# A recurrent decoder layer: both decay weights' arguments from one difference of running maximum and key, positive parts and parameters moved from VectorE to ScalarE

## The chip, the cores and the metric

The kernel runs on one core of one Trainium2 chip. The metric is the device time of one execution in microseconds (us), lower is better; times of a kernel are given as the median of several runs.

## What is computed

The program is one decoder block: four recurrent (RWKV) layers over x of 16 x 112 x 256 (batch, tokens, channels), then linear attention against a context of 16 x 375 x 256, then a dense mixture of eight experts. The change touches the recurrent layers only, in the recurrence that the reference calls wkv. Cut to that:

```python
w = -jnp.exp(time_decay); u = time_first          # one number per channel and layer
def step(carry, kv):
    aa, bb, pp = carry                            # numerator, denominator, running maximum
    kk, vv = kv
    ww = u + kk
    qq = jnp.maximum(pp, ww)
    e1 = jnp.exp(pp - qq); e2 = jnp.exp(ww - qq)
    out = (e1 * aa + e2 * vv) / (e1 * bb + e2)
    ww2 = pp + w
    qq2 = jnp.maximum(ww2, kk)
    e1b = jnp.exp(ww2 - qq2); e2b = jnp.exp(kk - qq2)
    return ((e1b * aa + e2b * vv, e1b * bb + e2b, qq2), out)
```

Around it each layer has two layer norms, three input mixes with their projections (key k, value v, gate r), an output projection, and a channel part (a hidden layer of 1024 with squared relu, and a gate).

## The kernel before

**Layout and steps.** The 16 sequences are cut into four groups of four. A group's working tiles are 128 channels x 2 channel halves (`CB`) x 4 sequences x 112 tokens, that is 128 partitions x 896 numbers, float32; an operation that needs a number per channel (bias, scale) has to be issued once per half, 128 x 448. Four layers by four groups are 16 units of work, m = 0 to 15; m // 4 is the layer. The order of the work is written out by hand, separately for each engine, in one loop over s = 0 to 16: while the channel part of unit s runs, the mixes, projections and recurrence of unit s + 2 are done, and the first norm of unit s + 3. Engines meet only through semaphores; each engine executes its own list strictly in order, so whatever waits holds back all that is behind it. Three warm-up units stand ahead of the loop.

**The recurrence of one unit** (lines 343 to 403 on VectorE, 652 to 671 on ScalarE). `pp` is the running maximum, made by one scan over the keys `kp` (L352). Then VectorE forms three arguments: `dp`, old maximum minus new maximum (L355); `dk`, key minus new maximum (L356); and `du` = key + u - old maximum (L359, one instruction per channel half because u differs by channel; it is put into the tile `rw`). ScalarE makes of them `e1b` = exp(dp + w) (L656, one per half, w as the bias), `e2b` = exp(dk) (L659), and `eu` = exp(u + key - old maximum), held below exp(24), as a Relu (L662) and an Exp (L664), each over the whole tile. VectorE's `wkv_sums` waits for e1b and e2b and runs the two scans `bb` (L366) and `aa` (L370); `wkv_denominator` (L375) waits for `eu`.

**The lists around it, in iteration s.**
- ScalarE, from the gate on: `gate(s)` (cth, L679, waits for TensorE's product with `wcr`), a table load (L761), `rsqrt0(1, s+3)` (L583, L585), `hidden(s, 0)` (L632, L634, L636: relu, square, rounded copy kfh), e1b, e2b of unit s + 2, `hidden(s, 1)`, `hidden(s, 2)`, a norm (L610 x4), eu, `hidden(s, 3)`, and then, in iteration s + 1, `rsqrt0(2, s+1)`: L583 `lnv` and L585 `y`.
- VectorE: `wkv_out`, `wkv_arguments` (L352 to L359), in some iterations a weight residue (L433, L440), `low_kf(s, 0)` (L421: the low part of the hidden values, kfl), the norm's four small operations (L274 to L286), `wkv_sums` (L366, L368, L370), `low_kf(s, 1)`, `low_kf(s, 2)`; then in iteration s + 1 `add_wkv` (L409), statistics (L268), the denominator (L375), L382, L383, the four small operations of the second norm (L274 waits for ScalarE's `y`), and `low_kf(s, 3)` (L421).
- TensorE, iteration s + 1: output projection `wo` (L809), the channel output in four quarters of 24 matmuls (L839; quarter p waits for kfl number p), with a transpose (L789) between, a second transpose, three projections (L799), the gate product `wcr` (L809), the hidden layer (L824).

So the fourth quarter of L839 can't start before VectorE's last `low_kf`, which stands behind L274, which waits for ScalarE's `y`, which stands behind all exponentials and hidden values of that iteration.

Layers' weights make the iterations differ by s % 4. When s % 4 is 0 (from s = 4 on) VectorE also computes two weight residues and ScalarE two weight copies (L643); at 2 and 3 one of each; at 1 none.

`prm` is the tile of the parameters per channel, with the columns of `NAMES`; columns from "w" on are computed at the start (L466 to L472 and L685).

Of the kernel before, what the change touches and what calls it, by code (L numbers as in the profile page):

```python
# [8 lines left out]
ACT = mybir.ActivationFunctionType  # L9
# [3 lines left out]
B, T, C = 16, 112, 256  # L13
L, F = 4, 1024
CB = C // P
# [3 lines left out]
T1 = T + 1  # L19
EPS = 1e-5  # L20
NEVER = -1e38
MOST = 24.0
UNIT = -0.5 / C
LN_EXP, EXP_TANH = "natural_log_exp_and_others", "exp_and_others"
FT = F // P
NAMES = ["ln1w", "ln1b", "tmk", "tmv", "tmr", "td", "u", "ln2w", "ln2b", "cmk", "cmr", "w", "pmk", "pmr"]
PRM = {n: i for i, n in enumerate(NAMES)}
NPRM, NPRM_IN = len(NAMES), NAMES.index("w")
S = 375
# [49 lines left out]
def rwkv_phase(nc, g, io, ctx):  # L79
# [11 lines left out]
    with tiles:  # L91
        def sb(name, shape, dt=FP32):
            return tiles.enter_context(nc.sbuf_tensor(name, shape, dt))

        def sem(name):
            return ctx.enter_context(nc.semaphore(name))
# [12 lines left out]
        prm = sb("prm", [P, L, CB, NPRM])  # L109
        eps, most = sb("eps", [P, 1]), sb("most", [P, 1])  # L110
# [18 lines left out]
        t = sb("kfl", [P, FT, G * T], F32R)  # L129
# [8 lines left out]
        kp = sb("kp", [P, CB, G, T1])  # L138
        v = sb("v", [P, CB, G, T])
        th = sb("th", [P, CB, G, T])  # L140
        pp = sb("pp", [P, CB, G, T1])
        reset = sb("reset", [P, G, T1])
        decay = sb("decay", [P, CB, G, T1])
        dp, dk = sb("dp", [P, CB, G, T]), sb("dk", [P, CB, G, T])
        diff = dk
        rw = [sb(f"rw{i}", [P, CB, G, T]) for i in range(2)]
        eu = sb("eu", [P, CB, G, T])
        e1b, e2b = sb("e1b", [P, CB, G, T1]), sb("e2b", [P, CB, G, T1])
# [8 lines left out]
        wexp_done, w_ready = sem("wexp_done"), sem("w_ready")  # L157
# [15 lines left out]
        arg_ready, side_ready, exp_ready = sem("arg_ready"), sem("side_ready"), sem("exp_ready")  # L173
# [72 lines left out]
        def vector(dve):  # L246
# [3 lines left out]
            def did(ins):  # L250
                ins.then_inc(dve_step, 1)
                steps[0] += 1
                return steps[0]

            def after(n):
                dve.wait_ge(dve_step, n)
# [5 lines left out]
            def param(m, b, name):  # L262
                return prm[:, m // GROUPS, b, PRM[name]:PRM[name] + 1]
# [33 lines left out]
            def input_stats(m):  # L297
                dve.wait_ge(x_in[m], 16)
                if m >= 2:

                    dve.wait_ge(shift_ready[0], m - 1)
                stats(0, chunk(m))
# [30 lines left out]
            def flat(t):  # L333
                return t[:].rearrange("p b g t -> p (b g t)")

            def at(t, first):

                return t[:, :, :, first:first + T].rearrange("p b g t -> p (b g) t")

            def tokens(t):  # L340
                return t[:].rearrange("p b g t -> p (b g) t")

            def wkv_arguments(m):
                n = 0
                if m % GROUPS == 0:
                    for b in range(CB):

                        n = did(dve.tensor_scalar(decay[:, b], reset[:], param(m, b, "w"), None, ALU.add))
                    after(n)
                dve.wait_ge(k_out, m + 1)  # L350

                n = did(dve.tensor_tensor_scan(flat(pp), flat(decay), flat(kp), 0.0, ALU.add, ALU.max))  # L352
                du = rw[m % 2]
                after(n)
                dve.tensor_tensor(tokens(dp), at(pp, 0), at(pp, 1), ALU.subtract).then_inc(arg_ready, 1)  # L355
                dve.tensor_tensor(tokens(dk), at(kp, 1), at(pp, 1), ALU.subtract).then_inc(arg_ready, 1)  # L356
                for b in range(CB):

                    dve.scalar_tensor_tensor(du[:, b], kp[:, b, :, 1:T1], param(m, b, "u"),  # L359
                                             pp[:, b, :, 0:T], ALU.add, ALU.subtract).then_inc(arg_ready, 1)  # L360

            def wkv_sums(m):


                dve.wait_ge(exp_ready, 4 * m + 3)
                did(dve.tensor_tensor_scan(flat(bb), flat(e1b), flat(e2b), 0.0, ALU.mult, ALU.add))  # L366
                dve.wait_ge(v_out, m + 1)
                n = did(dve.tensor_tensor(at(aa, 1), at(e2b, 1), tokens(v), ALU.mult))  # L368
                after(n)
                did(dve.tensor_tensor_scan(flat(aa), flat(e1b), flat(aa), 0.0, ALU.mult, ALU.add))  # L370

            def wkv_denominator(m):

                dve.wait_ge(exp_ready, 4 * m + 4)
                dve.tensor_tensor(tokens(dp), tokens(eu), at(bb, 0), ALU.add).then_inc(den_ready, 1)  # L375

            sums = {}
# [85 lines left out]

            dve.wait_ge(wexp_done, 1)
            pw = PRM["w"]
            dve.tensor_scalar(prm[:, :, :, pw:pw + 1], prm[:, :, :, pw:pw + 1], -1.0, None, ALU.mult).then_inc(w_ready, 1)  # L466
            for name in ("ln1w", "ln2w"):
                p = PRM[name]
                dve.tensor_scalar(prm[:, :, :, p:p + 1], prm[:, :, :, p:p + 1], UNIT, None, ALU.mult).then_inc(w_ready, 1)
            for name, mu in (("pmk", "cmk"), ("pmr", "cmr")):  # L470
                p, c = PRM[name], PRM[mu]
                dve.tensor_scalar(prm[:, :, :, p:p + 1], prm[:, :, :, c:c + 1], -1.0, 1.0, ALU.mult, ALU.add)\  # L472
                    .then_inc(w_ready, 1)
            dve.wait_ge(w_ready, 5)
            input_stats(0)
            rsqrt(0, 0)
            after(normalise(0, chunk(0)))
# [34 lines left out]
            for s in range(STEPS + 1):  # L512
# [40 lines left out]
                if valid(s + 2):  # L553
                    wkv_arguments(s + 2)
# [16 lines left out]
        def scalar(act):  # L571
            context_first, attention = g["attention"]["scalar"](act)

            def param(m, b, name):
                return prm[:, m // GROUPS, b, PRM[name]:PRM[name] + 1]
# [4 lines left out]
            def rsqrt0(k, m):  # L580

                act.wait_ge(lnstat[k], G // 2 * (m + 1))
                act.activation(lnv[k][:], m2[k], ACT.Ln, bias=eps[0:T, :], scale=1.0 / C).then_inc(lnlog[k], 1)  # L583
                act.wait_ge(lnlog[k], m + 1)
                act.activation(y0[k][:], lnv[k][:], ACT.Exp, scale=-0.5).then_inc(lny0[k], 1)  # L585
# [64 lines left out]
                act.activation(low[name][LOW[l][0]], stage[name][:, 0:HALF], ACT.Copy).then_inc(early_ready, 1)  # L650

            def wkv_exp(m, what):
                act.wait_ge(arg_ready, 4 * m + (what + 1 if what < 2 else 4))
                if what == 0:
                    for b in range(CB):
                        act.activation(e1b[:, b, :, 1:T1], dp[:, b], ACT.Exp, bias=param(m, b, "w"))\  # L656
                            .then_inc(exp_ready, 1)
                elif what == 1:
                    act.activation(e2b[:, :, :, 1:T1], dk[:], ACT.Exp).then_inc(exp_ready, 1)  # L659
                else:  # L660

                    act.activation(eu[:], rw[m % 2][:], ACT.Relu, bias=most[:], scale=-1.0).then_inc(side_ready, 1)  # L662
                    act.wait_ge(side_ready, m + 1)
                    act.activation(eu[:], eu[:], ACT.Exp, bias=most[:], scale=-1.0).then_inc(exp_ready, 1)  # L664

            def reciprocal0(m):
# [6 lines left out]
            def gate(m):  # L673

                act.wait_ge(cr_done, m + 1)
                if m:
# [5 lines left out]
            act.wait_ge(const_set, 12)  # L682
            act.wait_ge(params_in, 48)
            act.preload_act_table_set(LN_EXP)
            act.activation(prm[:, :, :, PRM["w"]:PRM["w"] + 1], prm[:, :, :, PRM["td"]:PRM["td"] + 1],  # L685
                           ACT.Exp).then_inc(wexp_done, 1)
            act.wait_ge(w_ready, 5)
            rsqrt0(0, 0)
            high_weights(0, "ck", wckh, ck_done, 4)
            rsqrt0(1, 0)  # L690
# [90 lines left out]
        def tensor(pe):  # L781
# [64 lines left out]
            for s in range(-3, STEPS + 1):  # L846
# [43 lines left out]
                if valid(m):  # L890
# [19 lines left out]
                    hidden(m, 3)  # L910

        return {"gpsimd": gpsimd, "sync": sync, "vector": vector, "scalar": scalar, "tensor": tensor}

def attention_phase(nc, g, io, ctx):
# [1172 lines left out]
```

## Time and profile before

| | us |
|---|---|
| median of 3 runs | 1837.98 (1837.52 to 1838.78) |
| the profiled execution's own time | 1839.21 |
| its span in the profile | 1837.5 |
| busy in the span: TensorE / VectorE / ScalarE | 1736.6 / 1242.6 / 977.0 |
| end of the recurrent layers in the profile | about 700 |

How to read it: the span is the time between first and last recorded instruction; the execution's own time is 1.7 us longer, what lies around the span. "Busy" sums recorded durations. In the profile's slices of the span VectorE is busy nine tenths or more in the recurrent part and about half in the experts; ScalarE's share falls likewise. A timeline row gives start, length, engine, line, and in brackets how long the engine had been idle before it and which engine and line released it. The length of a row that joins two instructions runs from the first's start to the second's end; instructions that follow each other on one engine overlap by about 0.1 us.

### The profile page before, as it was taken

Reading aid. Unit: us, or ns where it says so; the run is one execution under the profiler, and the core shown is the slowest. Engines: PE = TensorE matmul, PEld = TensorE weight load, DVE = VectorE, ACT = ScalarE, POOL = GpSimd, SP = SyncE. Lnnn points to the kernel's source line nnn. Section 1 sums busy time; section 2 is a strip of 40 time slices with the busy share of each in tenths; the row PEclk is TensorE's granted clock in tenths of the full one; section 3 lists DMA queues with packets and bytes.
Section 4 is the critical chain, followed back from the end, with each engine's and each line's share of the span. In section 5 each row is a group of like instructions: output and inputs, shape, how many; then the busy total and the mean of one; then the engine's idle time right before and its main releaser. Section 6 shows DMA issues by size and latency. Waiting matters only on the chain.

```text
span 1837.5 us, 27225 instructions
## 1 busy us (share of the span) xinstructions
PE 1736.6 (95%) x10508; PEld 1520.3 (83%) x10508; DVE 1242.6 (68%) x1918; ACT 977.0 (53%) x1505; POOL 3.6 (0%) x26
## 2 busy tenths in 40 slices
PE   3599999999999998998999999999999999999997
PEld 1378888778888788888899889998999989999896
DVE  7999999999999855888554445444454544445446
ACT  4688898898989773444533333333333332333323
POOL 0000000000000000000000000000000000000000
PEclk9799999999999998999999999999999999999999
DMA  4000010001000002111111010000011001120001
GB/s 143 1 25 17 12 47 18 7 8 62 1 12 29 0 30 89 44 55 45 55 35 35 1 35 35 34 33 2 34 34 34 11 23 34 34 74 0 1 1 41
DMA packets 34702, 56.59 MB, mean 31 GB/s; under 512 B 3030, under 2 KB 20412, under 8 KB 33596
## 3 DMA queue, kind: packets, MB, share of 16 engines
q1 hardware_dynamic: 34620, 55.47, 9.3%
q8 instruction: 55, 0.90, 0.2%
q14 instruction: 27, 0.22, 0.0%
HBM read 51.79 MB, written 3.67 MB: 30 GB/s over the span
## 4 chain that ended last, share of the span: by engine, by line
PE 70%; DVE 24%; ACT 3%; issue 2%; DMA 0%; SPq 0%; ACTq 0%; DVEq 0%
PE fbank L1935 33%; PE fbank L1957 17%; PE pair L839 5%; PE pair L799 4%; PE pair L824 3%; DVE kfl L421 2%; PE proj L1429 2%; PE pair L809 2%; DVE st L268 2%; DVE aa L370 1%; DVE bb L366 1%; DVE pp L352 1%; PE qbanks L1465 1%; PE pair L789 1%; DVE x L409 1%
## 5 line engine op out<-in xcount | busy, mean ns | idle before, releaser
L1757 DVE TENSOR_TENSOR hf<-sil,fbank 128x512 f32<-128x512 f32 (+1 forms) x256 | 158.8, 620 | 479.2 <-PE fbank L1935 407.5
L1862 ACT ACTIVATE sil<-fbank 128x512 f32<-128x512 f32 (+1 forms) x256 | 139.2, 544 | 615.1 <-PE fbank L1935 615.1
L1935 PE MATMUL fbank<-xh,wh 128*128 128x512 f32 (+1 forms) x1024 | 289.8, 364 | 1.2 <-ACT sil L1862 1.2
L1935 PE MATMUL fbank<-xl,wh 128*128 128x512 f32 (+1 forms) x1024 | 289.0, 363 | 0.0
L1935 PE MATMUL fbank<-xh,wl 128*128 128x512 f32 (+1 forms) x1024 | 288.9, 363 | 0.0
L1957 PE MATMUL fbank<-wl,hh 128*128 128x256 f32 x896 | 250.3, 279 | 0.0
L1957 PE MATMUL fbank<-wh,hh 128*128 128x256 f32 x896 | 250.2, 279 | 0.0
L1957 PE MATMUL fbank<-wh,hl 128*128 128x256 f32 x896 | 250.1, 279 | 0.0
L1935 PEld LDWEIGHTS fbank<-xl,wh 128*128 128x128 f32 x1024 | 184.6, 189 | 30.8
L1935 PEld LDWEIGHTS fbank<-xh,wl 128*128 128x128 f32 x1024 | 184.4, 189 | 30.4
L1935 PEld LDWEIGHTS fbank<-xh,wh 128*128 128x128 f32 x1024 | 180.5, 189 | 27.8 <-ACT sil L1862 1.6
L1957 PEld LDWEIGHTS fbank<-wl,hh 128*128 128x128 f32 x896 | 168.3, 188 | 2.1
L1957 PEld LDWEIGHTS fbank<-wh,hh 128*128 128x128 f32 x896 | 168.4, 188 | 1.8
L1957 PEld LDWEIGHTS fbank<-wh,hl 128*128 128x128 f32 x896 | 168.4, 188 | 0.0
L1764 DVE TENSOR_TENSOR hl<-hf,hh 128x512 fp32r<-128x512 f32 (+1 forms) x256 | 158.1, 618 | 0.0
L839 PE MATMUL pair<-wcvh,kfh 128*112 128x256 f32 x512 | 148.7, 291 | 9.8 <-DVE kfl L421 9.2
L1855 ACT ACTIVATE hh<-hf 128x512 fp32r<-128x512 f32 (+1 forms) x256 | 146.0, 570 | 0.5 <-DVE hf L1757 0.5
L839 PE MATMUL pair<-wcvh,kfl 128*112 128x256 f32 x512 | 143.8, 281 | 0.0
L839 PE MATMUL pair<-wcvl,kfh 128*112 128x256 f32 x384 | 107.6, 280 | 0.0
L839 PEld LDWEIGHTS pair<-wcvh,kfh 128*112 128x112 f32 x512 | 89.7, 175 | 13.5 <-DVE kfl L421 12.8
L839 PEld LDWEIGHTS pair<-wcvh,kfl 128*112 128x112 f32 x512 | 89.7, 175 | 0.0
L1781 DVE SCALAR_TENSOR_TENSOR acc<-fbank,cw,acc 128x256 f32<-128x256 f32 x210 | 87.3, 475 | 0.0
(239 smaller groups left out, 3109.6 us busy)
## 6 DMA issues: line engine op xcount, KB each, us to landing
raw<-in_w_gate SPq DMA_DIRECT2D x16, 512.0 KB, 3.8
raw<-in_w_up SPq DMA_DIRECT2D x16, 512.0 KB, 4.7
raw<-in_w_down SPq DMA_DIRECT2D x16, 512.0 KB, 5.7
raw<-in_w_ck SPq DMA_DIRECT2D x4, 1024.0 KB, 4.8
raw<-in_w_cv SPq DMA_DIRECT2D x4, 1024.0 KB, 4.8
raw<-in_ctx_t SPq DMA_DIRECT2D x4, 750.0 KB, 5.9
ct<-in_ctx_t SPq DMA_DIRECT2D x4, 750.0 KB, 4.9
x<-in_x SPq DMA_DIRECT2D x4, 448.0 KB, 6.9
```

Source lines behind the costliest of these rows:

```text
L268: dve.bn_stats(st[k][:, i, :], xc[:, 2 * i:2 * i + 2, :].rearrange("p g c -> p c g"))\
L421: dve.tensor_tensor(kfl[j], kf[j], kfh[:, 2 * j:2 * j + 2], ALU.subtract)\
L799: ins = pe.matmul(pair[KVR[which]][:, o, 0:G * T], w[:, b, o * P:(o + 1) * P], src[:, b].rearrange("p g t -> p (g t)"), start=b == 0, stop ...
L824: ins = pe.matmul(banks[:, i, 0:G * T], w[b], a[:, b, :], start=n == 0, stop=n == 3 * CB - 1)
L839: ins = pe.matmul(pair[3][0:T, i // 2, (i % 2) * C:(i % 2 + 1) * C], a[:, i * T:(i + 1) * T], w, start=j == n == i % 2 == 0, stop=j == FT ...
L1757: dve.tensor_tensor(hf[i][:, 0:w], sil[i][:, 0:w], banks(e, t, f)[1][:, 0:w], ALU.mult).then_inc(hf_ready, 1)
L1764: dve.tensor_tensor(hl[t % 2][:, f, 0:w], hf[f % 2][:, 0:w], hh[t % 2][:, f, 0:w], ALU.subtract)\
L1781: ins = dve.scalar_tensor_tensor(a, ps, w, a, ALU.mult, ALU.add)
L1855: act.activation(hh[t % 2][:, f, 0:w], hf[f % 2][:, 0:w], ACT.Copy).then_inc(hh_ready, 1)
L1862: act.activation(sil[f % 2][:, 0:w], banks(e, t, f)[0][:, 0:w], ACT.Silu).then_inc(sil_ready, 1)
L1935: ins = pe.matmul(banks(e, t, f)[k][:, 0:w], m[h][:, o:o + P], a[:, b, columns(c)], start=i == 0, stop=i == 3 * CB - 1)
L1957: ins = pe.matmul(bank[4 + 2 * (t % 2) + i // 2][:, (i % 2) * C:(i % 2 + 1) * C], a[t % 2][:, f, i * P:(i + 1) * P], m[h][:, DOWN + f * C: ...
```

## The change

On VectorE, `dp` becomes old maximum minus key, and `du` is no longer computed (two instructions less for each unit). On ScalarE both e1b and eu start from dp. With we = exp(time_decay) = -w, the new maximum is the larger of old maximum + w and key, so the argument of e1b is -max(0, we - dp): one Relu for each half with bias we and scale -1, then one Exp with scale -1 over the whole tile. The argument of eu is 24 - max(0, 24 - u + dp): one Relu for each half with bias 24 - u, then the Exp as before. The semaphores' counts follow. At the start one more small VectorE instruction makes the column 24 - u.

```diff
-NAMES = ["ln1w", ..., "cmr", "w", "pmk", "pmr"]
+NAMES = ["ln1w", ..., "cmr", "w", "we", "mostu", "pmk", "pmr"]
...
                 n = did(dve.tensor_tensor_scan(flat(pp), flat(decay), flat(kp), 0.0, ALU.add, ALU.max))
-                du = rw[m % 2]
                 after(n)
-                dve.tensor_tensor(tokens(dp), at(pp, 0), at(pp, 1), ALU.subtract).then_inc(arg_ready, 1)
+                dve.tensor_tensor(tokens(dp), at(pp, 0), at(kp, 1), ALU.subtract).then_inc(arg_ready, 1)
                 dve.tensor_tensor(tokens(dk), at(kp, 1), at(pp, 1), ALU.subtract).then_inc(arg_ready, 1)
-                for b in range(CB):
-                    dve.scalar_tensor_tensor(du[:, b], kp[:, b, :, 1:T1], param(m, b, "u"),
-                                             pp[:, b, :, 0:T], ALU.add, ALU.subtract).then_inc(arg_ready, 1)
...
-                dve.wait_ge(exp_ready, 4 * m + 3)
+                dve.wait_ge(exp_ready, 3 * m + 2)
...
-                dve.wait_ge(exp_ready, 4 * m + 4)
+                dve.wait_ge(exp_ready, 3 * m + 3)
...
-            dve.tensor_scalar(prm[:, :, :, pw:pw + 1], prm[:, :, :, pw:pw + 1], -1.0, None, ALU.mult).then_inc(w_ready, 1)
+            pe, pu, pm = PRM["we"], PRM["u"], PRM["mostu"]
+            dve.tensor_scalar(prm[:, :, :, pw:pw + 1], prm[:, :, :, pe:pe + 1], -1.0, None, ALU.mult).then_inc(w_ready, 1)
+            dve.tensor_scalar(prm[:, :, :, pm:pm + 1], prm[:, :, :, pu:pu + 1], -1.0, MOST, ALU.mult, ALU.add)\
+                .then_inc(w_ready, 1)
...
             def wkv_exp(m, what):
-                act.wait_ge(arg_ready, 4 * m + (what + 1 if what < 2 else 4))
+                def over(out, name, scale):
+                    for b in range(CB):
+                        act.activation(out[:, b], dp[:, b], ACT.Relu, bias=param(m, b, name), scale=scale)\
+                            .then_inc(side_ready, 1)
+                per = 2 * CB
                 if what == 0:
-                    for b in range(CB):
-                        act.activation(e1b[:, b, :, 1:T1], dp[:, b], ACT.Exp, bias=param(m, b, "w"))\
-                            .then_inc(exp_ready, 1)
+                    act.wait_ge(arg_ready, 2 * m + 1)
+                    t = e1b[:, :, :, 1:T1]
+                    over(t, "we", -1.0)
+                    act.wait_ge(side_ready, per * m + CB)
+                    act.activation(t, t, ACT.Exp, scale=-1.0).then_inc(exp_ready, 1)
                 elif what == 1:
+                    act.wait_ge(arg_ready, 2 * m + 2)
                     act.activation(e2b[:, :, :, 1:T1], dk[:], ACT.Exp).then_inc(exp_ready, 1)
                 else:
-                    act.activation(eu[:], rw[m % 2][:], ACT.Relu, bias=most[:], scale=-1.0).then_inc(side_ready, 1)
-                    act.wait_ge(side_ready, m + 1)
+                    over(eu, "mostu", 1.0)
+                    act.wait_ge(side_ready, per * (m + 1))
                     act.activation(eu[:], eu[:], ACT.Exp, bias=most[:], scale=-1.0).then_inc(exp_ready, 1)
```

What the engines' lists show. VectorE after the scan `pp` of unit 3 (iteration s = 1), before:

```order
L355 TENSOR_TENSOR dp<-pp 128x896 [waits dve_step]
L356 TENSOR_TENSOR dk<-kp,pp 128x896
L359 SCALAR_TENSOR_TENSOR rw<-kp,prm,pp 128x448 x2
L421 TENSOR_TENSOR kfl<-kf,kfh 128x896 [waits kfh_ready]
L274 TENSOR_TENSOR yy<-y 112x4 [waits lny01]
```

and now:

```order
L354 TENSOR_TENSOR dp<-pp,kp 128x896 [waits dve_step]
L355 TENSOR_TENSOR dk<-kp,pp 128x896
L416 TENSOR_TENSOR kfl<-kf,kfh 128x896 [waits kfh_ready]
L274 TENSOR_TENSOR yy<-y 112x4 [waits lny01]
```

The two half-tile instructions that made `du` are gone; nothing else moves. ScalarE between the first hidden values and the second, same iteration, before:

```order
L636 ACTIVATE kfh<-kf 128x896 [waits square_done]
L656 ACTIVATE e1b<-dp,prm 128x4x112 [waits arg_ready]
L656 ACTIVATE e1b<-dp,prm 128x4x112
L659 ACTIVATE e2b<-dk 128x8x112 [waits arg_ready]
L632 ACTIVATE kf<-pair 128x896 [waits ck_done]
```

and now:

```order
L634 ACTIVATE kfh<-kf 128x896 [waits square_done]
L654 ACTIVATE e1b<-dp,prm 128x4x112 [waits arg_ready]
L654 ACTIVATE e1b<-dp,prm 128x4x112
L663 ACTIVATE e1b<-e1b 128x8x112 [waits side_ready]
L666 ACTIVATE e2b<-dk 128x8x112 [waits arg_ready]
L630 ACTIVATE kf<-pair 128x896 [waits ck_done]
```

One whole-tile Exp, which waits for the two Relus (`side_ready`), now stands ahead of e2b. Further down the eu pair, before:

```order
L610 ACTIVATE xn<-x,shift,rstd 112x256 x3
L662 ACTIVATE eu<-rw,most 128x896 [waits arg_ready]
L664 ACTIVATE eu<-eu,most 128x896 [waits side_ready]
L632 ACTIVATE kf<-pair 128x896 [waits ck_done]
```

and now:

```order
L608 ACTIVATE xn<-x,shift,rstd 112x256 x3
L654 ACTIVATE eu<-dp,prm 128x448 x2
L670 ACTIVATE eu<-eu,most 128x896 [waits side_ready]
L630 ACTIVATE kf<-pair 128x896 [waits ck_done]
```

The whole-tile Relu has become two of half the size. TensorE's list is the same.

## Rows read from the trace of the kernel before

**Rows 1.** Busy time in one whole layer: stretch, each engine's busy us, clock
```profile
285.18:443.12 157.94, 155.15 (x865) 128.51 (x865) 153.10 (x199) 139.55 (x189) 0.00 (x0) 1.00 0.07 22
```
**Rows 2.** TensorE timeline: first matmul of the fourth L839 quarter, s % 4 = 0, 1, 2, 3
```profile
281.33 0.37 PE L839 MATMUL pair<-wcvh,kfh 128*112 128x256 f32 x1 [1.63 <-DVE kfl L421]
...
319.90 0.37 PE L839 MATMUL pair<-wcvh,kfh 128*112 128x256 f32 x1
...
359.62 0.37 PE L839 MATMUL pair<-wcvh,kfh 128*112 128x256 f32 x1 [0.93 <-DVE kfl L421]
...
556.38 0.37 PE L839 MATMUL pair<-wcvh,kfh 128*112 128x256 f32 x1
```
**Rows 3.** Waits between 200 and 660 us: total us, times, longest
```profile
ACT cth L679 <- PE pair L809: 20.4, 9, 2.9
...
DVE mix_ck L330 <- ACT mix_ck L601: 3.9, 11, 0.4
```
**Rows 4.** Chain of waits: VectorE's du pair
```profile
538.06 1.19 DVE rw L359 x2
```
**Rows 5.** Groups of instructions, ScalarE, to 800 us: busy us, mean ns
```profile
L656 ACT ACTIVATE e1b<-dp,prm 128x448 f32<-128x448 f32 x32 | 19.5, 656 | 2.6 <-DVE dp L355 2.6
...
L671 ACT ACTIVATE e1b<-e2b 128x896 f32<-128x896 f32 x16 | 15.3, 955 | 0.5
```
**Rows 6.** ScalarE timeline, iteration s = 5 (s % 4 = 1)
```profile
303.27 1.22 ACT L656 ACTIVATE e1b<-dp,prm 128x448 f32<-128x448 f32 x2
304.39 0.95 ACT L659 ACTIVATE e2b<-dk 128x896 f32<-128x896 f32 x1
...
312.74 1.03 ACT L662 ACTIVATE eu<-rw,most 128x896 f32<-128x896 f32 x1
313.80 1.05 ACT L664 ACTIVATE eu<-eu,most 128x896 f32<-128x896 f32 x1
...
317.85 0.20 ACT L585 ACTIVATE y<-lnv 112x4 f32<-112x4 f32 x1
```
**Rows 7.** VectorE timeline, iteration s = 5
```profile
305.37 2.04 DVE L366 TENSOR_TENSOR_SCAN bb<-e1b,e2b 128x904 f32<-128x904 f32 x1 [0.21 <-ACT e2b L659]
...
318.09 0.16 DVE L274 TENSOR_TENSOR yy<-y 112x4 f32<-112x4 f32 x1
...
318.76 1.08 DVE L421 TENSOR_TENSOR kfl<-kf,kfh 128x896 fp32r<-128x896 f32 x1
```
**Rows 8.** y and the L274 behind it: s = 4, 6, 11 (s % 4 = 0, 2, 3)
```profile
277.07 0.20 ACT L585 ACTIVATE y<-lnv 112x4 f32<-112x4 f32 x1
279.53 0.15 DVE L274 TENSOR_TENSOR yy<-y 112x4 f32<-112x4 f32 x1
...
356.44 0.20 ACT L585 ACTIVATE y<-lnv 112x4 f32<-112x4 f32 x1
357.82 0.16 DVE L274 TENSOR_TENSOR yy<-y 112x4 f32<-112x4 f32 x1
...
554.07 0.20 ACT L585 ACTIVATE y<-lnv 112x4 f32<-112x4 f32 x1
554.58 0.15 DVE L274 TENSOR_TENSOR yy<-y 112x4 f32<-112x4 f32 x1
```
**Rows 9.** The same two instructions in iteration s = 0
```profile
120.07 0.20 ACT L585 ACTIVATE y<-lnv 112x4 f32<-112x4 f32 x1
121.64 0.15 DVE L274 TENSOR_TENSOR yy<-y 112x4 f32<-112x4 f32 x1
```
**Rows 10.** Warm-up, units 0 and 1: e2b and the scan bb behind it
```profile
38.91 0.94 ACT L659 ACTIVATE e2b<-dk 128x896 f32<-128x896 f32 x1
40.51 2.03 DVE L366 TENSOR_TENSOR_SCAN bb<-e1b,e2b 128x904 f32<-128x904 f32 x1
...
67.75 0.93 ACT L659 ACTIVATE e2b<-dk 128x896 f32<-128x896 f32 x1
70.66 2.04 DVE L366 TENSOR_TENSOR_SCAN bb<-e1b,e2b 128x904 f32<-128x904 f32 x1
```

More of the change, by code:

```diff
@@ L25 @@
 FT = F // P
-NAMES = ["ln1w", "ln1b", "tmk", "tmv", "tmr", "td", "u", "ln2w", "ln2b", "cmk", "cmr", "w", "pmk", "pmr"]
+NAMES = ["ln1w", "ln1b", "tmk", "tmv", "tmr", "td", "u", "ln2w", "ln2b", "cmk", "cmr", "w", "we", "mostu", "pmk", "pmr"]
 PRM = {n: i for i, n in enumerate(NAMES)}
@@ L473, in vector @@
                     .then_inc(w_ready, 1)
-            dve.wait_ge(w_ready, 5)
+            dve.wait_ge(w_ready, 6)
             input_stats(0)
@@ L684, in scalar @@
             act.preload_act_table_set(LN_EXP)
-            act.activation(prm[:, :, :, PRM["w"]:PRM["w"] + 1], prm[:, :, :, PRM["td"]:PRM["td"] + 1],
+            act.activation(prm[:, :, :, PRM["we"]:PRM["we"] + 1], prm[:, :, :, PRM["td"]:PRM["td"] + 1],
                            ACT.Exp).then_inc(wexp_done, 1)
-            act.wait_ge(w_ready, 5)
+            act.wait_ge(w_ready, 6)
             rsqrt0(0, 0)
```

## The prediction

> **What bounds the kernel now.** I read the busy times by stretch first. In one whole layer of 157.94 us TensorE is busy 155.15, VectorE 153.10 and ScalarE 139.55, at a granted clock of 1.00 [rows 1]. By that table VectorE is nearly full and relieving it should pay, but TensorE is nearly full too. So the second view is TensorE's timeline, for where it stands still. It does so in one place of an iteration, ahead of the fourth quarter of L839, and always for VectorE's last kfl: 1.63 us when s % 4 is 0, 0.93 when it is 2, under the list's threshold at 1 and 3 (at 3 the start at 556.38 is still the end of kfl) [rows 2]. Those gaps are the most that a faster VectorE could win in the loop. The third view is the waits: ScalarE's gate L679 waits for TensorE's product in nine iterations, and VectorE's mix_ck for ScalarE in eleven [rows 3]. So once per iteration both are set back to TensorE's time, and what they save or lose before that goes on only through the kfl for which TensorE waits. I therefore follow one chain: TensorE's gate product, ScalarE from gate through hidden values and exponentials to the norm's y (L585), VectorE's L274, last kfl, TensorE.
>
> **What is removed.** VectorE's du pair takes 1.19 us of each of 16 units [rows 4]. In the loop it stands ahead of L366, which waits for e2b. In s = 5 e2b ends at 304.39 + 0.95 = 305.34 and L366 starts at 305.37 [rows 6, 7]: there VectorE is waiting already, and the saving is nothing. dp reads another tile in the same shape; I cost that at nothing, since its start is hidden behind ScalarE's hidden values: e1b starts only at 303.27.
>
> **What is added on ScalarE.** First e1b. Before: two half-tile Exps, and e2b starts 1.12 after the first (303.27, 304.39) [rows 6]. Now two half-tile Relus with a bias from a tile, as the old Exps had (0.656 each, 1.22 together) [rows 5, 6], then an Exp that waits for them, then e2b. A dependent instruction starts some 0.03 after the end of what it reads (L664 at 313.80, after 312.74 + 1.03) [rows 6]. An Exp over the whole tile without a bias tile takes 0.955, as L671 [rows 5], and the next starts about 0.09 before its end (two of 0.656 take 1.22 [rows 5, 6]). So e2b starts 1.22 + 0.03 + 0.86 = 2.11 after the first Relu, 0.99 later than before. Second eu. Before: the Exp starts 1.06 after the Relu (312.74, 313.80) [rows 6]; now 1.22 + 0.03 = 1.25 after the first of two: 0.19 more. Together ScalarE gets 1.18 us longer between gate and y, in each unit. Bounds: if the Exp starts without the dependency's wait and overlaps fully, and the eu halves cost only the extra overlap, 1.0; if the Exp costs like L664 (1.05) [rows 6] and both dependencies 0.05 more, 1.37.
>
> The Trainium skill, "ScalarE: Activation LUTs", section "Rules for kernel authors", says to run relu, add and mul on VectorE and not here, which speaks against the change. The rows don't show the reason it gives (speed per element): half a tile costs 1.19 / 2 = 0.60 on VectorE and 0.56 to 0.66 here. By either price the work is about even; what decides is whose time is waited for.
>
> **Iteration by iteration.** L274 starts about 0.04 after y's end (317.85 + 0.20, 318.09), and the last kfl starts 0.67 after it and takes 1.08: 319.84, when TensorE starts at 319.90 [rows 2, 6, 7]. With y 1.18 later:
> - **s % 4 = 1** (1, 5, 9, 13). L274 waits for y already, so all 1.18 arrives. In some of the four TensorE had a few hundredths in hand, and in the last the norm on ScalarE falls away and only e1b's 0.99 counts; I take 1.1 each: +4.4.
> - **s % 4 = 2** (2, 6, 10). y's end goes from 356.64 to 357.82, L274 from 357.82 to 357.86 [rows 8]. VectorE's own saving is eaten by e2b and eu on the way. +0.04 each: +0.1.
> - **s % 4 = 3** (3, 7, 11). y's end goes from 554.27 to 555.45, L274 from 554.58 to 555.49 [rows 8]: +0.9 each, +2.7.
> - **s % 4 = 0** (4, 8, 12). Here VectorE is late because of two weight residues. y's end goes from 277.27 to 278.45, L274 from 279.53 to 278.49 [rows 8]: -1.04 of the 1.63 that TensorE waits, and VectorE's own 1.19 allows it. -3.1.
> - **s = 0**: y's end from 120.27 to 121.45, L274 from 121.64 to 121.49 [rows 9]: -0.15.
>
> The loop's sum is 4.4 + 0.1 + 2.7 - 3.1 - 0.15 = +3.95. Each of these lets gate, mix_ck and the projections move with TensorE, so the terms add.
>
> **Warm-up.** TensorE and ScalarE have much idle time there, VectorE sets the pace. Unit 0: e2b ended at 39.85 and L366 started at 40.51, after the du pair. Now e2b ends at 40.84, so L366 comes 0.36 later [rows 10]. The added instruction on 8 numbers per partition costs 0.1 more. Unit 1 then starts 0.45 late: e2b ends at 68.68 + 0.45 + 0.99 = 70.12, L366 starts at 70.15, where it stood at 70.66, since the du pair no longer fills the time [rows 10]. So the loop begins 0.5 us earlier. Nothing in attention or experts is touched; they move with the end of the recurrence.
>
> **Sum.** 3.95 - 0.5 = **+3.4 us**: 1842.6 for the profiled execution of 1839.21, which stood 1.2 above the median of 1837.98. Against the median the forecast is **1841.4 us**, 0.19% slower. A measurement of this kernel can tell about 0.2% (3.7 us) from no change, so the likeliest result lies just inside that border.
>
> **Rivals.**
> - **The VectorE saving passes through (faster).** If the Relus and the Exp overlap so that e2b comes no later, L366 and L274 start up to 1.19 earlier and TensorE wins what it waited: 1.19 at s % 4 = 0, 0.93 at 2, up to 0.3 at 3, nothing at 1, some 2.4 a layer, 7 in three layers, about 1.2 at s = 0 and 2.4 in the warm-up. That gives -11: 1827. For it: VectorE's 97% [rows 1]. Against it: L366 releasing directly on e2b in s = 5 [rows 7], with an Exp more in front. 5 in 100. The Trainium skill, "Perfetto Trace Analysis", "Identifying the Most-Contended Engine", would point here: optimise the engine of highest occupancy first. By busy time that is VectorE rather than ScalarE's 88%, and the trace agrees on the shares; it disagrees on who is waited for.
> - **ScalarE's chain is dearer (clearly slower).** The place is the pair Relu, Exp on e1b in place, in strided rows, and the same on eu. At 1.5 instead of 1.18 each of 14 iterations gives 0.32 more: +4.5, together +7.9, 1845.9. It decides early: 0.02 us more for each iteration carries the result over 3.7 us. For it: no row shows a Relu of half a tile out of VectorE's tile with its Exp behind it. Against: L656, L662 and L671 are that form in everything but one point each [rows 5, 6]. 10 in 100.
> - **ScalarE's addition is cheaper.** At 0.8 instead of 1.18, -0.38 in 14 iterations is -5.3: -1.9, 1836. It would need the Exp to cost 0.6. 7 in 100.
>
> **How the numbers follow.** The forecast's case has 78 in 100. Inside it the bounds 1.0 and 1.37 give 14 x -0.18 = -2.5 and 14 x 0.19 = +2.7, so 1838.9 to 1844.1, and 46 in 100 of it lie beyond +3.7. Slower by over 0.2%: 0.78 x 0.46 + 0.10 = 0.46. Faster: 0.05. Within 0.2%: the rest, 0.42 + 0.07 = 0.49. The range goes from 1837.3 (half the way into the cheap case) to 1844.9 (half the way into the dear one); the faster case and the ends of both others are left out.
>
> **What the profile after should show.** VectorE's busy time in the span down by about 32 x 0.6 = 19 us or a little more, ScalarE's up by about 20 (0.955 for the Exp and 0.28 for a Relu in two halves, 16 times). VectorE waits for e2b ahead of L366 in nearly every iteration, for about 1 to 2 us, and for y ahead of the second norm's L274 in all. TensorE's wait ahead of the fourth L839 quarter: 0.6 (1.63 - 1.04) at s % 4 = 0, 1.1 at 1, 1.0 at 2, 1.2 at 3; its wait in all becomes more even. A whole layer takes 157.94 + 0.04 + 0.9 + 1.15 - 1.04 = about 159 us. Three things would prove me wrong: L366 starting without a wait; e2b starting less than 2.0 or more than 2.3 after the first Relu; iterations with s % 4 = 1 not growing.

## The result, and the profile after

The change makes the kernel slower by 0.3%: 1844.13 us (median of 9 runs, 1842.28 to 1844.80) against 1837.98 (9 runs, 1836.29 to 1839.11), ratio 1.0032 with an interval of 1.0023 to 1.0042. The forecast was 1841.4, inside a range of 1837.3 to 1844.9. So the sign was right, and the size was 6.2 us where 3.4 was forecast. The forecast gave 46 in 100 to a result slower by over 0.2%, which is what came, and 49 to one within 0.2%. A second comparison (after_again, below) gave 1842.23.

The profiled execution took 1844.8 us (span 1842.7; before 1839.21 and 1837.5). What lies outside the span has grown too: 2.1 us in each of the 16 runs of the changed kernel (2.04 to 2.14), where 54 runs of the kernel before in the later comparisons have 1.7 (1.67 to 1.80). du_kept and e1b_only, which keep the du pair, have 1.7 as well, and the kernels without it 1.9 to 2.2, so these 0.4 us go with its removal; why, no run shows. Section 1 of the page after, and the chain that ended last by engine, followed by that chain on the page before:

```profile
PE 1738.1 (94%) x10508; PEld 1519.7 (82%) x10508; DVE 1226.3 (67%) x1887; ACT 994.3 (54%) x1537; POOL 3.6 (0%) x26
...
PE 71%; DVE 14%; ACT 13%; issue 2%; DMA 0%; SPq 0%; ACTq 0%; DVEq 0%
```
```profile
PE 70%; DVE 24%; ACT 3%; issue 2%; DMA 0%; SPq 0%; ACTq 0%; DVEq 0%
```
VectorE has 16.3 us less work than before (1242.6) where 19 was forecast, ScalarE 17.3 more (977.0) where 20 was. Ten points of the span have gone from VectorE to ScalarE in the chain (24% to 14%, 3% to 13%).

TensorE's timeline after, first matmul of the fourth quarter for s % 4 = 0, 1, 2, 3 and 0 again, which answers to [rows 2]:

```profile
283.34 0.37 PE L845 MATMUL pair<-wcvh,kfh 128*112 128x256 f32 x1 [0.90 <-DVE kfl L416]
...
323.07 0.38 PE L845 MATMUL pair<-wcvh,kfh 128*112 128x256 f32 x1 [0.99 <-DVE kfl L416]
...
362.81 0.38 PE L845 MATMUL pair<-wcvh,kfh 128*112 128x256 f32 x1 [0.96 <-DVE kfl L416]
...
402.56 0.38 PE L845 MATMUL pair<-wcvh,kfh 128*112 128x256 f32 x1 [0.96 <-DVE kfl L416]
...
442.32 0.38 PE L845 MATMUL pair<-wcvh,kfh 128*112 128x256 f32 x1 [0.94 <-DVE kfl L416]
```
The reader is to see the equal steps: 39.73, 39.74, 39.75, 39.76 us. Before, they were unequal: 281.33 to 319.90 is 38.57, to 359.62 is 39.72 [rows 2], and the next two starts give 38.83 and 40.80:

```profile
398.45 0.37 PE L839 MATMUL pair<-wcvh,kfh 128*112 128x256 f32 x1
...
439.25 0.37 PE L839 MATMUL pair<-wcvh,kfh 128*112 128x256 f32 x1 [1.58 <-DVE kfl L421]
```
Iterations that were short have grown, the long one has shrunk, and TensorE waits 0.9 to 1.0 us in each. The layer between the same matmuls:

```profile
283.34:442.32 158.98, 155.13 (x864) 128.07 (x865) 149.11 (x191) 143.84 (x197) 0.00 (x0) 1.00 0.07 22
```
158.98 us, as forecast (159), at a granted clock of 1.00. VectorE went from 153.10 to 149.11, ScalarE from 139.55 to 143.84 [rows 1]. Why the steps are equal is seen on the two engines in s = 5. ScalarE's timeline after, to set against [rows 6]:

```profile
305.28 1.21 ACT L654 ACTIVATE e1b<-dp,prm 128x448 f32<-128x448 f32 x2
306.53 0.95 ACT L663 ACTIVATE e1b<-e1b 128x896 f32<-128x896 f32 x1
307.39 0.94 ACT L666 ACTIVATE e2b<-dk 128x896 f32<-128x896 f32 x1
...
315.74 1.21 ACT L654 ACTIVATE eu<-dp,prm 128x448 f32<-128x448 f32 x2
316.99 1.04 ACT L670 ACTIVATE eu<-eu,most 128x896 f32<-128x896 f32 x1
...
321.02 0.20 ACT L583 ACTIVATE y<-lnv 112x4 f32<-112x4 f32 x1
```
e2b starts 2.11 us after the first Relu and the second eu 1.25 after the first: both as forecast. From the first Relu to y it is 15.74 us; before, from the first Exp to y, 14.58: 1.16 more, where 1.18 was forecast. VectorE's timeline after, against [rows 7]:

```profile
308.36 2.04 DVE L361 TENSOR_TENSOR_SCAN bb<-e1b,e2b 128x904 f32<-128x904 f32 x1 [1.20 <-ACT e2b L666]
...
321.26 0.16 DVE L274 TENSOR_TENSOR yy<-y 112x4 f32<-112x4 f32 x1
...
321.93 1.08 DVE L416 TENSOR_TENSOR kfl<-kf,kfh 128x896 fp32r<-128x896 f32 x1
```
The scan bb, which had waited 0.21 here, waits 1.20: 0.99 more, exactly what e2b is later behind the first Relu. Over all units that wait grew from 1.5 us to 14.2; groups of instructions, before and then after (last column: idle time ahead):

```profile
L366 DVE TENSOR_TENSOR_SCAN bb<-e1b,e2b 128x904 f32<-128x904 f32 x16 | 32.6, 2036 | 1.5 <-ACT e2b L659 1.5
```
```profile
L361 DVE TENSOR_TENSOR_SCAN bb<-e1b,e2b 128x904 f32<-128x904 f32 x16 | 32.6, 2040 | 14.2 <-ACT e2b L666 14.2
```
VectorE got 16.3 us less work and 12.7 us more waiting at this one place (and 6.1 more ahead of its kfl, for ScalarE's kfh: 17.4 to 23.5).

The 5.2 us by which the span grew divide so. The first and the last of the fourth quarters, of before and then of after:

```profile
123.44 0.37 PE L839 MATMUL pair<-wcvh,kfh 128*112 128x256 f32 x1 [1.15 <-DVE kfl L421]
...
635.26 0.37 PE L839 MATMUL pair<-wcvh,kfh 128*112 128x256 f32 x1 [0.17 <-DVE kfl L421]
```
```profile
124.38 0.37 PE L845 MATMUL pair<-wcvh,kfh 128*112 128x256 f32 x1 [0.90 <-DVE kfl L416]
...
640.37 0.38 PE L845 MATMUL pair<-wcvh,kfh 128*112 128x256 f32 x1 [1.16 <-DVE kfl L416]
```
Up to the first of them +0.94, between them 515.99 - 511.82 = +4.17, behind them +0.1. The forecast had -0.65 (warm-up and s = 0), +4.1 and 0. **The loop is right, and the warm-up has the wrong sign.**

The warm-up lost in TensorE's projections by mix_k of units 1 and 2. Their rows in TensorE's timeline, of before and then of after:

```profile
50.76 5.18 PE L799 MATMUL pair<-mix_k,wk 128*128 128x448 f32 x8 [4.84 <-DVE mix_k L323]
85.70 4.73 PE L799 MATMUL pair<-mix_k,wk 128*128 128x448 f32 x8
```
```profile
51.17 5.92 PE L805 MATMUL pair<-mix_k,wk 128*128 128x448 f32 x8 [4.26 <-DVE mix_k L323]
85.95 5.55 PE L805 MATMUL pair<-mix_k,wk 128*128 128x448 f32 x8
```
And busy times by stretch, TensorE alone (stretch, its length, busy us, granted clock), before and then after:

```profile
44.00:50.00 6.00, 1.73 (x8) 0.50 0.00 0
50.00:58.00 8.00, 7.24 (x14) 0.71 0.00 0
...
88.00:92.00 4.00, 4.00 (x11) 0.90 0.02 4
```
```profile
44.00:50.00 6.00, 1.73 (x8) 0.50 0.00 0
50.00:58.00 8.00, 6.83 (x11) 0.59 0.00 0
...
88.00:92.00 4.00, 4.00 (x8) 0.66 0.02 4
```
The same eight matmuls take 3.19 us in the loop, at a granted clock of 1.00. Here they take 5.18 and 4.73 before, 5.92 and 5.55 after. Ahead of them TensorE had mostly stood idle (4.84 and 4.26 us on mix_k alone), and from 44 to 50 us the granted clock was 0.50, the 1.2 GHz level; by the means of the stretches it rose somewhere within the projection. In TensorE's timeline a weight load takes 0.34 us up to 53.9 us and 0.19 from 55.0 on before, 0.34 up to 55.8 and 0.19 from 56.9 on after: the clock rose later. Unit 2's projection starts 0.25 us later than before and is 0.82 longer; less the 0.15 of s = 0 that is +0.92, the measured +0.94.

### The profile page after: what moved, and what is told of

It reads as the page before. It is cut to its first block, busy times and chain, and to the rows that moved or that the text cites. A ratio compares the mean times of both kernels' runs of the same rounds, so it can differ in the third digit from the quotient of the medians.

```text
span 1842.7 us, 27226 instructions
## 1 busy us (share of the span) xinstructions
PE 1738.1 (94%) x10508; PEld 1519.7 (82%) x10508; DVE 1226.3 (67%) x1887; ACT 994.3 (54%) x1537; POOL 3.6 (0%) x26
## 4 chain that ended last, share of the span: by engine, by line
PE 71%; DVE 14%; ACT 13%; issue 2%; DMA 0%; SPq 0%; ACTq 0%; DVEq 0%
PE fbank L1941 33%; PE fbank L1963 17%; PE pair L805 7%; PE pair L845 3%; PE pair L815 3%; PE proj L1435 2%; ACT kf L632 2%; ACT kfh L634 2%; ACT kf L630 1%; ACT xn L608 1%; DVE kfl L416 1%; PE pair L830 1%; DVE st L268 1%; PE qbanks L1471 1%; DVE rw L378 1%
```

## The experiments

The first question was whether the chain of the forecast holds when parts of the change are undone.

**du_kept**: the change, with the du pair left on VectorE although nobody reads what it writes.

```diff
+                du = rw[m % 2]
+                for b in range(CB):
+                    dve.scalar_tensor_tensor(du[:, b], kp[:, b, :, 1:T1], param(m, b, "u"),
+                                             pp[:, b, :, 0:T], ALU.add, ALU.subtract)
```


> The changed kernel, with the du pair put back on VectorE behind dk (its result is not used), so VectorE's load is as before and ScalarE's as after. Theory (one chain from TensorE's gate product over ScalarE's y to the last kfl, TensorE waits for it): iterations with s % 4 = 0 go back from 39.74 to about 40.8 us, the others stay at 39.7 to 39.75; about 3.5 us slower than the changed kernel, 9 to 10 slower than before (ratio 1.005). Rival (VectorE's whole load counts): 16 x 1.19 = 19 us slower than the changed kernel. Rival (only ScalarE's load counts): same as the changed kernel.

Measured 1847.38 us (5 runs) beside 1838.45 for before: ratio 1.0048 (1.0035 to 1.0062), +8.9 where 9 to 10 was expected, and 3.3 above the changed kernel (3.5 expected). TensorE's fourth quarters, s % 4 = 0 and 1:

```profile
284.59 0.38 PE L849 MATMUL pair<-wcvh,kfh 128*112 128x256 f32 x1 [1.65 <-DVE kfl L420]
...
324.34 0.37 PE L849 MATMUL pair<-wcvh,kfh 128*112 128x256 f32 x1 [0.90 <-DVE kfl L420]
```
Steps of 39.75 three times, and 40.78 at s % 4 = 0 with its old wait of 1.65. So what the removed pair gives in the changed kernel is 1.0 at s % 4 = 0 (40.78 against 39.76) and nothing at 1, 2 and 3. Both rivals fall.

**e1b_only**: dp, the Relu pair and the Exp for e1b as in the change, du and eu as before (the semaphores' counts follow).

```diff
-                dve.tensor_tensor(tokens(dp), at(pp, 0), at(pp, 1), ALU.subtract).then_inc(arg_ready, 1)
+                dve.tensor_tensor(tokens(dp), at(pp, 0), at(kp, 1), ALU.subtract).then_inc(arg_ready, 1)
...
-                        act.activation(e1b[:, b, :, 1:T1], dp[:, b], ACT.Exp, bias=param(m, b, "w"))\
-                            .then_inc(exp_ready, 1)
...
+                    t = e1b[:, :, :, 1:T1]
+                    over(t, "we", -1.0)
+                    act.wait_ge(side_ready, per * m + CB)
+                    act.activation(t, t, ACT.Exp, scale=-1.0).then_inc(exp_ready, 1)
```


> Only the first half of the change: dp as old maximum minus key, e1b by two Relus and one Exp; du and eu as before. ScalarE 0.99 us longer per unit, VectorE unchanged. Theory: s % 4 = 1 grows by 1.0, 3 by 0.7, 2 and 0 by nothing, so +6 in the loop and about +0.5 in the warm-up: 6.5 us slower than before, a little slower than the changed kernel. Rival (the warm-up costs 1.5 us by itself as in the changed kernel's profile, whatever the cause): 7.5 to 8.

Measured 1845.52 us, ratio 1.0037 (1.0023 to 1.0051), +7.1, between the 6.5 expected and the rival's 7.5 to 8. The step at s % 4 = 1 is 39.55 to 39.58 us (before 38.57 to 38.64): 0.92 to 1.01 more, where e1b's own is 0.99. At 3 it is 39.54 instead of 38.83 (0.7, as expected), at 2 and 0 unchanged, and the loop from first to last fourth quarter grew by 6.0. In du_kept, where eu's 0.19 comes on top, the step at s % 4 = 1 is 39.75. So what is added on ScalarE is paid nearly in full there.

**no_du**: the other half alone. before without the du pair; eu reads dk, so u and the old maximum are left out of eu's argument, while ScalarE's instructions keep their number and shape.

```diff
-                for b in range(CB):
-                    dve.scalar_tensor_tensor(du[:, b], kp[:, b, :, 1:T1], param(m, b, "u"),
-                                             pp[:, b, :, 0:T], ALU.add, ALU.subtract).then_inc(arg_ready, 1)
...
-                    act.activation(eu[:], rw[m % 2][:], ACT.Relu, bias=most[:], scale=-1.0).then_inc(side_ready, 1)
+                    act.activation(eu[:], dk[:], ACT.Relu, bias=most[:], scale=-1.0).then_inc(side_ready, 1)
```


> The kernel before without the du pair; eu reads dk instead, so u and its argument are left out of the computation. ScalarE's load as before, VectorE's 1.19 us less per unit. Theory: s % 4 = 0 shrinks by 1.2, 2 by 0.93 (all that TensorE waited), 3 by 0.3, 1 by nothing, -7.2 in three layers, -1.1 in s = 0, -1.8 in the warm-up: 10 us faster than before (1828). Rival (nothing to win on VectorE, TensorE bounds): within 2 us of before.

Measured 1827.42 us, ratio 0.9942 (0.9928 to 0.9955): 11.0 us faster, 10 expected. In the trace the fourth quarter shows a wait for kfl only once in a layer, at s % 4 = 0:

```profile
275.54 0.37 PE L834 MATMUL pair<-wcvh,kfh 128*112 128x256 f32 x1 [0.81 <-DVE kfl L416]
```
This is the price of the first rival (-11), reached where ScalarE is charged nothing. VectorE's 1.19 us is worth 11 us by itself; the change pays 1.18 us of ScalarE for it and loses all of that and 4 to 6 us more.

**pool_du** tries to have the one without the other, with nothing left out: VectorE's du pair is gone, GpSimd forms key minus old maximum for the whole tile, and ScalarE takes u in the two halves of eu's Relu (`over` is the change's pair of half-tile Relus, reading `rw` here).

```diff
+            for m in range(STEPS):
+                pool.wait_ge(arg_ready, 2 * m + 1)
+                pool.tensor_tensor(flat(rw[m % 2], 0), flat(kp, 1), flat(pp, 0), ALU.subtract).then_inc(du_ready, 1)
...
-                    act.activation(eu[:], rw[m % 2][:], ACT.Relu, bias=most[:], scale=-1.0).then_inc(side_ready, 1)
+                    act.wait_ge(du_ready, m + 1)
+                    over(eu, "mostu", -1.0)
```


> A version with the reference's result: dp, e1b, e2b as before, key minus old maximum by one whole-tile subtraction on GpSimd, u as the bias of two half-tile Relus on ScalarE. VectorE 1.19 us less, ScalarE 0.19 more per unit. Theory: s % 4 = 0: -1.19, 1: +0.19, 2: -0.93, 3: -0.1, s = 0: -1.1, warm-up -1.8: 8 to 9 us faster than before. Rival (VectorE's instructions slow down while GpSimd works in the same memory): each unit loses up to 1 us on VectorE and the gain falls to 0 to 4 us.

Measured 1848.69 us, ratio 1.0057 (1.0043 to 1.0070), 10 us slower, where 8 to 9 faster was expected and the rival still gave a gain of 0 to 4. GpSimd and VectorE in s = 4:

```profile
267.04 1.08 DVE L363 TENSOR_TENSOR dk<-kp,pp 128x896 f32<-128x896 f32 x1
267.20 2.92 POOL L210 TENSOR_TENSOR rw<-kp,pp 128x896 f32<-128x896 f32 x1 [38.62 <-DVE dp L362]
268.04 3.16 DVE L436 TENSOR_TENSOR wcvl<-raw,wcvh 128x1024 fp32r<-128x1024 f32 x1
```
The weight residue took 3.16 us, where the same operation takes 1.22 undisturbed: it ends 1.08 after GpSimd's does. dk at 267.04 kept its 1.08. I read that as contiguous operations being held back and strided ones not, and moved GpSimd's work beside the scans.

**pool_du2** is that: the same kernel with `pool.wait_ge(exp_ready, 3 * m + 2)` in place of the wait on arg_ready. The expectation's "e1b pair as in the change" doesn't describe it: e1b is two Exps from dp, as before, in all kernels with GpSimd.

> As pool_du (e1b pair as in the change, the difference of key and old maximum by GpSimd, both halves of eu by ScalarE), but GpSimd starts its 2.9 us when the scans bb and aa start, not beside the residue and kfl. Theory (only VectorE's contiguous subtractions of two SBUF tiles are held back, scans and strided operations are not): VectorE has 1.2 us a unit less and loses nothing, so 6 to 10 us faster than before, 1828 to 1832. Rival (the scans or the kfl behind them are held back by 2 to 3 us as well): 3 to 12 us slower than before, 1841 to 1850.

Measured 1860.18 us (4 runs), ratio 1.0121 (1.0106 to 1.0137): 22 us slower, beyond even the rival's figures. The same two engines in s = 5:

```profile
314.35 2.04 DVE L369 TENSOR_TENSOR_SCAN bb<-e1b,e2b 128x904 f32<-128x904 f32 x1 [0.21 <-ACT e2b L672]
...
316.31 2.91 DVE L371 TENSOR_TENSOR aa<-e2b,v 128x896 f32<-128x896 f32 x1
```
```profile
314.40 3.88 POOL L210 TENSOR_TENSOR rw<-kp,pp 128x896 f32<-128x896 f32 x1 [39.02 <-ACT e2b L672]
```
My reading falls: the product aa is strided, and it took 2.91 us instead of 1.07. The rows fit another one. bb began first and kept its 2.04; GpSimd's subtraction, begun 0.05 later, took 3.88, which is bb's time and some 1.9 of its own; the product ends 0.94 behind it. In another unit GpSimd began first (71.81), and there bb took 3.80. The shortest of the 16 subtractions, 2.14, is one that began ahead of a VectorE instruction on four numbers per partition, which takes 0.16 elsewhere and took 2.06 behind it:

```profile
111.35 2.14 POOL L210 TENSOR_TENSOR rw<-kp,pp 128x896 f32<-128x896 f32 x1 [37.13 <-ACT e2b L672]
111.46 2.06 DVE L294 SCALAR_TENSOR_TENSOR shift<-st,rstd 112x4 f32<-112x4 f32 x1
```
So in these rows whichever starts first keeps its time, and the other waits it out. By the Trainium skill, "SBUF — State Buffer", section "SBUF: two separate sides", the pair of ports that both engines share is an exclusive lock for a whole instruction, taken by GpSimd and, where GpSimd's instruction reads SBUF as here, by those VectorE instructions that have two SBUF inputs (or run in a two-port mode). These rows agree on the waiting (2.04 and 3.88, 2.14 and 2.06); that the ports are its cause no run here shows. In this kernel most of VectorE's work around the recurrence reads two SBUF tiles, so the 1.19 us taken from it bring back a wait of up to 1.9.

**The warm-up.** Does the excess over the forecast come from the granted clock of the cold projections? If so, it goes when TensorE is kept busy ahead of them. Four kernels give both versions useless products in TensorE's idle stretches.

```diff
+            def busy(n):
+                for _ in range(n):
+                    pe.matmul(pair[3][:, 0, 0:448], ident[:], reset[:].rearrange("p g t -> p (g t)")[:, 0:448],
+                              start=True, stop=True)
...
+                    busy({0: 20, 1: 14, 2: 11}.get(m, 0))
                     turn(1, m, pair[2])
+                    busy({1: 6}.get(m, 0))
...
+                    busy({0: 14}.get(m, 0))
                     turn(2, m, pair[0])
```


> The kernel before with products of no use (20, 14, 6, 11 and 14 matmuls of 128x448 on constant tiles into an unused bank) put into TensorE's idle time of the warm-up, so that its granted clock is still high when the projections of units 1 and 2 come. Theory: the mix_k projection in the warm-up takes 3.0 us instead of 4.6 to 5.9, and the time falls by 2 to 4 us. Rival (the warm-up is VectorE's alone): no change. If the products themselves delay TensorE: slower.

> The changed kernel with the same products. If the changed kernel's extra 1.5 us of the warm-up is a matter of TensorE's clock there, this stands 3.5 to 4.5 us above the kernel before with the same products. Rival (the extra is a wait that the change makes): 5.5 to 6.5 above it.

Measured: before_warm 1836.97 (11 runs), ratio 0.9995 (0.9986 to 1.0004) to the kernel before (1837.76, 24 runs beside it); after_warm 1842.69 (6 runs), ratio 1.0030 (1.0018 to 1.0042) to the same. The granted clock was 1.00 from 44 to 92 us in both traces, and the projections of units 1 and 2 took the 3.19 of the loop. The one of unit 0, ahead of them, did not. Unit 0's of before_warm, then those of the three units in after_warm:

```profile
25.56 5.55 PE L804 MATMUL pair<-mix_k,wk 128*128 128x448 f32 x8 [3.09 <-DVE mix_k L323]
```
```profile
24.83 4.69 PE L810 MATMUL pair<-mix_k,wk 128*128 128x448 f32 x8 [3.09 <-DVE mix_k L323]
...
51.20 3.17 PE L810 MATMUL pair<-mix_k,wk 128*128 128x448 f32 x8
85.29 3.19 PE L810 MATMUL pair<-mix_k,wk 128*128 128x448 f32 x8
```
Yet before_warm gained 0.8 us by the medians (the interval goes from 2.6 faster to 0.7 slower), not 2 to 4: I had taken half of what one such product costs (it takes 0.75 us), and they held back the transposes behind them. From 44 to 92 us TensorE is now busy 47.0 of 48.0 us in both traces, so this pair doesn't show any more what VectorE and ScalarE do in the warm-up. The change's fourth quarters run from 121.34 to 637.45 and before's from 123.07 to 634.86: +4.3 in the loop, and -1.7 ahead of it. Of these 0.7 lie ahead of the first transposes (20.76 and 21.48), 0.86 in the first projection (4.69 and 5.55, at a mean granted clock of 0.72 from 25 to 30 us and 0.65 from 26 to 32), and 0.15 in s = 0; nothing is left for the forecast's term. The medians' difference, 5.7, lies in the rival's range (5.5 to 6.5, "a wait that the change makes") and not in the 3.5 to 4.5 of a clock. But the two profiled executions differ by 1.7 only: they are the slowest of eleven and the fastest of six. So it took another pair.

**before_again and after_again** (unchanged kernels) show how much of it is scatter.

> The kernel before once more, for a second trace of its warm-up: if the clock's rise in the three cold projections falls at a random point, their lengths (5.85, 5.02 and 4.56 us in the first trace) differ here by some tenths to 0.8 us. Rival: they repeat, since the schedule sets them.

> The changed kernel once more, for a second trace of its warm-up (5.07, 5.76 and 5.39 us in the first). Theory of a random point: lengths differ, first matmul of the fourth quarter in s = 1 at 123 to 125 us. Rival: they repeat and it starts at 124.4 again.

Measured 1838.29 (10 runs) and 1842.23 (7 runs; its ratio to the 24 runs of before beside it, median 1837.76, is 1.0029, 1.0017 to 1.0040). The loop again grew by 4.2 (123.12 to 639.03 us, against 122.94 to 634.67). The projections took 6.14 and 3.97 us after, 4.80 and 4.35 before: unlike those of the first pair, in the same kernels, so both rivals ("they repeat") fall. Between the two traces of before all three differ by 0.4; between those of after, unit 2's differs by 1.6.

**before_warm2 and after_warm2** have fewer products (7 and 3 around unit 1's transposes, 6 ahead of unit 2's, 6 ahead of the second transposes of s = 0).

> The kernel before with fewer useless products in the idle stretches of TensorE's warm-up (0.75 us each: 7 and 3 around unit 1's transposes, 6 ahead of unit 2's, 6 ahead of the second transposes of s=0; none that can hold back the first transposes). Theory: the eight mix_k projections of units 1 and 2 then take about 3.0 us each time where the kernel before shows 4.2 to 5.0 in all, and the first 4th quarter starts 1 to 3 us earlier than in the kernel before: 1835 to 1837 us. Rival: filling costs as much as it brings, as in before_warm: 1837 to 1839.

> The change with the same products. Theory (the part of the change's cost beyond 3.4 us is TensorE's lower granted clock in the cold projections of the warm-up): 3 to 4 us above before_warm2, with the two kernels' mix_k projections of equal length. Rival (it is a wait that the change itself brings in the warm-up): 5.5 to 6 us above before_warm2.

Measured (11 runs each) 1838.11, ratio to before 1.0002 (0.9993 to 1.0011), and 1841.35, ratio 1.0020 (1.0011 to 1.0029). before_warm2 missed the 1 to 3 us that it was to gain. Its granted clock was 1.00 from 44 to 50 us and 0.57 from 50 to 58: the products ahead of it did not hold the clock through unit 1's projection. The difference, 3.2 us, is inside the 3 to 4 expected, but not for the reason given, since the projections were not of equal length:

```profile
50.78 6.26 PE L804 MATMUL pair<-mix_k,wk 128*128 128x448 f32 x8 [3.40 <-DVE mix_k L323]
85.73 4.10 PE L804 MATMUL pair<-mix_k,wk 128*128 128x448 f32 x8
...
122.84 0.37 PE L844 MATMUL pair<-wcvh,kfh 128*112 128x256 f32 x1 [1.11 <-DVE kfl L421]
```
```profile
50.92 3.25 PE L810 MATMUL pair<-mix_k,wk 128*128 128x448 f32 x8 [1.17 <-DVE mix_k L323]
83.94 3.19 PE L810 MATMUL pair<-mix_k,wk 128*128 128x448 f32 x8
...
119.99 0.38 PE L850 MATMUL pair<-wcvh,kfh 128*112 128x256 f32 x1 [0.94 <-DVE kfl L416]
```
In this pair the change's trace had the high clock and reached its loop 2.85 us earlier; its unit 2 projection started 1.79 earlier, was 0.91 shorter, and s = 0 gave 0.15. The loop grew by 4.3 once more.

**pool_du2_warm2** has both edits.

> pool_du2 with the products of before_warm2. Theory: the two add up, 1 to 3 us under pool_du2. Rival: within 0.5 us of pool_du2.

Measured 1858.06 us (4 runs), 2.1 under pool_du2: its loop starts 3.0 earlier in the trace (124.84 against 127.84), and the two edits add. No version that leaves nothing out beat before by more than its interval.

## Why the forecast came out as it did

**Held, with sizes.** The chain (gate, ScalarE, y, L274, kfl, TensorE) and its terms in the loop. The iterations, as steps between fourth quarters, before and after: s % 4 = 1, 38.57 to 39.73, +1.16 (forecast 1.1); 2, 39.72 to 39.74, +0.02 (0.04); 3, 38.83 to 39.75, +0.92 (0.9); 0, from 40.80 to 39.76, -1.04 (-1.04). The loop from first to last fourth quarter: +4.17, +4.18, +4.32 and +4.31 in four pairs of traces, +4.1 forecast. du_kept and e1b_only put each term where the forecast had it. TensorE's waits were 0.9, 1.0, 1.0 and 1.0 where 0.6, 1.1, 1.0 and 1.2 stood: the sum is right, the division is not. With y as the last wait in all four kinds of iteration they have become alike, in their waits as in their lengths. VectorE's wait ahead of bb was 0.5 to 1.9 us in 13 units ("about 1 to 2" in the forecast) and too short to be listed in the three at s % 4 = 0 (4, 8, 12).

**Failed: the warm-up term.** "TensorE and ScalarE have much idle time there, VectorE sets the pace", so "the loop begins 0.5 us earlier". bb of unit 0 started at 40.91 us (forecast 40.87), as reckoned. bb of unit 1 started at 70.92 where 70.15 was forecast: the projection ahead of it took 5.92 us instead of 5.18, so ScalarE came to the e1b pair at 67.78 and not at 67.09 (66.64 + 0.45), and e2b ended 0.7 later. Then unit 2's projection took 0.82 more. From -0.65 these two steps, 0.77 and 0.82, lead to the measured +0.94. The forecast had taken the length of the projections as fixed, without a reason. It isn't: after TensorE had stood idle its granted clock was 0.50, and the projections were in the path at 4 to 6 us each instead of 3.19. In the profiles the loop's start moved by +0.94, +0.18, -1.7 and -2.85 in the four pairs. The lengths of the projections have their part in each: in the second pair unit 1's is 1.34 longer and unit 2's 0.38 shorter, in the third unit 0's is 0.86 shorter, in the fourth unit 1's 3.01 and unit 2's 0.91. That the forecast's -0.65 is hidden beneath this scatter can be neither shown nor ruled out from these traces. The forecast also had nothing for the 0.4 us outside the span.

**Left open.** The medians' differences in the four pairs are 6.2, 3.9, 5.7 and 3.2 us, where the loop accounts for 4.2 to 4.3 and the time outside the span for 0.4. Their sum, 4.6, lies inside the intervals of both comparisons of the unchanged kernels (4.2 to 7.7 and 3.1 to 7.4 us); the forecast's 3.4 lies inside the second only. What remains, -1.5 to +1.6, has the size of the clock's scatter in single executions, which the end of the kernel has too: from the last of those fourth quarters to the end of the span it is 1200.9 to 1202.3 us in the eight traces, and one group of twelve matmuls there (kvp, at 713 to 720 us) took 2.95 us in three of them and 1.61 in five, at a granted clock of 0.50 in after and 0.92 in after_again. Whether the change shifts the moment at which the clock rises on average, or only that of single executions, no run here tells. For a shift speaks that unit 1's projection took 5.79 to 6.24 us in all four traces with the Exp added and without useless products (after, after_again, du_kept, e1b_only) and 5.18 and 4.80 in the two of before; against it, that no_du, with ScalarE's list as before, has 6.04. Holding the clock up in both kernels did not bring the medians to the forecast, so that cause is shown for single traces and only argued for the 6.2.

**The rivals.** The dear chain (1.5 us instead of 1.18, 1845.9) gives the measured total nearly, and is refuted all the same: 1.16 was seen. "The VectorE saving passes through" fell for the change and came true in no_du. The rule to optimise the engine of highest occupancy first (the Trainium skill, "Perfetto Trace Analysis", "Identifying the Most-Contended Engine") was half right here: VectorE's relief is worth 11 us by itself (no_du), but ScalarE, with 88%, stands in the path as well, and what is given to it comes back in the time (e1b_only, +7.1).

## What to carry to other kernels

Where two engines take turns on one chain within an iteration, moving work between them isn't priced by their busy shares: take each engine's saving and addition from the wait that ends last in each kind of iteration, of which there were four here. Measure the two halves of an exchange apart (-11 us for the one, +7 for the other) before judging it. And look what a third engine does to the second before counting its work as free: here GpSimd's subtraction held VectorE up, and the kernels with it were 10 and 22 us slower.

## What was unexpected of the hardware

GpSimd's subtraction of 128x896 f32 took 2.14 us at its shortest and up to 3.94 where a VectorE instruction had begun before it; a VectorE instruction with two SBUF inputs behind it took up to 1.9 us longer (1.07 to 2.91, 1.22 to 3.16, 2.04 to 3.80, and 0.16 to 2.06 on four numbers per partition). Whichever began first kept its time. And the same eight projections in the same kernel took 3.97 to 5.55 us in two executions (85 to 92 us), at a mean granted clock of 0.80 and 0.59 there. In this kernel a forecast for the warm-up is uncertain by that much.
